# First input rows and first weights of the expert stage fetched ahead of the out projection's end

## The reference, cut to what matters

```python
    y = ys.transpose(1, 0, 2) + D_skip * xi
    y = y * jax.nn.silu(z)
    return y @ out_proj_w                      # the out projection
...
    h = residual + h
    residual = h
    h = rmsnorm(h, rms2_w)
    # moe_block: top 2 of 8 experts of each token
    for e in range(N_EXPERTS):
        w_e = jnp.where(sel == e, top_w, 0.0).sum(axis=-1)
        ye = jax.nn.silu(hs @ Wg[e]) * (hs @ Wu[e]) @ Wd[e]
        out = out + w_e[:, None] * ye
```

## Time and profile before

| | |
|---|---|
| median of 3 runs | 713.15 us (712.68 to 714.09) |
| the profiled execution, whole | 710.69 us |
| its span, first to last instruction | 708.9 us |
| busy: PE, DVE, ACT, POOL | 572.2, 483.9, 387.6, 324.7 us |
| mean granted clock of PE | 0.939 of 2.4 GHz |
| the chain that ended last | PE 40%, DVE 9%, issue 6%, ACT 4% of the span |

### The profile page before, as it was taken

How to read it: one execution, slowest core, us unless ns; L and a number is a source line. 1 busy time by engine, 2 the same in 40 slices (tenths; PEclk the granted TensorE clock), 3 DMA queues, 4 the chain that set the end, 5 groups by cost and what they waited for, 6 DMA issues and landing times.

```text
span 708.9 us, 11068 instructions
## 1 busy us (share of the span) xinstructions
PE 572.2 (81%) x3444; PEld 363.5 (51%) x3463; DVE 483.9 (68%) x1294; ACT 387.6 (55%) x618; POOL 324.7 (46%) x285
## 2 busy tenths in 40 slices
PE   3956889986795567788789999956789989988787
PEld 1412334442342222778789999933545545545466
DVE  4769999938999987444223655388687778887052
ACT  2675666666643553464356656523266566566741
POOL 5268989809895996225648332433012103112010
PEclk9979999997878988998899999976999999999999
DMA  5855556325774652300141201323103003000001
GB/s 146 292 168 158 156 167 190 113 63 177 235 224 148 177 164 67 87 19 32 46 117 34 82 21 32 108 82 81 35 2 106 10 3 106 3 3 1 3 15 46
DMA packets 50524, 65.92 MB, mean 93 GB/s; under 512 B 7730, under 2 KB 29250, under 8 KB 50210
## 3 DMA queue, kind: packets, MB, share of 16 engines
q1 hardware_dynamic: 45122, 59.27, 28.5%
q0 software_dynamic: 2496, 5.15, 2.0%
q10 hardware_dynamic: 2848, 0.78, 0.5%
HBM read 47.46 MB, written 9.52 MB: 80 GB/s over the span
## 4 chain that ended last, share of the span: by engine, by line
PE 40%; DVE 9%; issue 6%; ACT 4%; another core or an unknown queue 1%; ACTq 1%; POOL 0%; DMA 0%; POOLq 0%; DVEq 0%
PE ps L1643 37%; DVE arena L1563 3%; ACT arena L1163 2%; PE ps L1957 1%; DVE x L1498 1%; DVE nb L1262 1%; DVE stats L1249 1%; PE ps L1964 1%; PE ps L1847 1%; ACTq L1153 1%; ACT arena L1183 0%; ACT r L1163 0%; ACT arena L1171 0%; DVE mv L1252 0%
## 5 line engine op out<-in xcount | busy, mean ns | idle before, releaser
L1643 PE MATMUL ps<-arena 128*128 128x128 f32 (+12 forms) x2147 | 336.2, 333 | 53.5 <-DVE arena L1563 17.9
L1643 PEld LDWEIGHTS ps<-arena 128*128 128x128 f32 (+4 forms) x2166 | 214.6, 160 | 142.4 <-issue 65.1
L1643 PE MATMUL ps<-arena,ident 128*128 128x512 f32 x256 | 134.0, 664 | 46.4 <-DVE arena L1446 46.4
L1434 DVE TENSOR_TENSOR_SCAN arena<-ps,arena 128x512 f32<-128x512 f32 x128 | 149.4, 1211 | 13.3 <-ACT ps L1091 6.8
L859 POOL TENSOR_TENSOR arena<-arena 128x1024 f32<-128x1024 f32 x64 | 126.9, 1998 | 40.8 <-DVE arena L1421 38.4
L1091 ACT ACTIVATE ps<-arena 128x512 f32<-128x512 f32 x128 | 87.5, 690 | 79.3 <-DVE arena L1434 74.3
L1563 DVE CUSTOM_DVE_ANT_0 arena<-ps,cmask 128x128 f32<-128x128 f32 (+3 forms) x256 | 111.5, 488 | 26.5 <-PE ps L1643 25.4
L1643 PEld LDWEIGHTS ps<-arena,ident 128*128 128x128 f32 x256 | 51.5, 211 | 123.1 <-DVE arena L1446 68.3
L1617 DVE TENSOR_TENSOR arena<-arena,ps 128x512 f32<-128x512 f32 x46 | 31.7, 689 | 78.0 <-PE ps L1643 35.8
L846 POOL DMA_INDIRECT moe_out<-arena,xT x46 | 45.5, 988 | 82.7 <-DVE arena L1587 72.3
L1163 ACT ACTIVATE arena<-ps 128x1024 f32<-128x1024 f32 (+3 forms) x86 | 57.1, 709 | 36.0 <-PE ps L1643 35.6
(11 more groups left out here) (200 smaller groups left out, 609.9 us busy)
## 6 DMA issues: line engine op xcount, KB each, us to landing
arena<-bc_rows SPq DMA_DIRECT2D x128, 256.0 KB, 3.7
arena<-arena SPq DMA_DIRECT2D x64, 64.0 KB
arena<-arena SPq DMA_DIRECT2D x28, 128.0 KB, 2.4
moe_rows<-arena SPq DMA_DIRECT2D x2, 1495.0 KB, 11.9
arena<-moe_rows SPq DMA_DIRECT2D x8, 325.0 KB, 4.2
arena<-in_L_attn_a_Wg SPq DMA_DIRECT2D x8, 256.0 KB, 4.4
arena<-in_L_attn_a_Wu SPq DMA_DIRECT2D x8, 256.0 KB, 5.0
arena<-moe_out SPq DMA_DIRECT2D x4, 512.0 KB, 4.4
```

What stands on the lines that cost most here:

```text
L1434: V.tensor_tensor_scan(hst[:, g % STATES, e, :], bank(6 + e), dBx[:, g % RING, e, :], 0.0, ALU.mult, ALU.add).then_inc(s_scan, 1)
L1643: return T.matmul(o, l, rr, start=start, stop=stop)
```

## The change

Four things are done.

- `load_blocks(0)` no longer waits for `s_op` ahead of its first two transfers (blocks 0 to 7), but for `s_dx` at 4 and `s_ys` at 49, the last reads of `xc`, whose memory these blocks fill. From the third transfer on it waits for `s_op` as before. `load_blocks(1)` loses the wait for `s_op`, which stands ahead of it on the queue.
- ACT copies the first block's weights once all products with C are done (`s_hc`, `s_hp`), since these were the last reads of the scan states.
- `out_proj(1, block_turn)` turns block 0 between its two sequences and block 1 behind the second.
- The two turns behind the out projection are gone; the wait for the experts' weights stays and now stands ahead of PE's register load.

```diff
@@ -191,6 +191,7 @@
         CH = (0, 3, 8, 13, 18, NBLK)
+        EARLY = 2
@@ -268,6 +269,7 @@
         xg0 = carve([NBLK, NROW])
+        assert rows_at + CH[EARLY] * NROW <= moe_from + CT * HL
@@ -698,9 +700,13 @@
             def load_blocks(h):
-                sp.wait_ge(s_op, NB)
                 sp.wait_ge(s_sc[h], 16 * 2 * TH)
+                if h == 0:
+                    sp.wait_ge(s_dx, NB)
+                    sp.wait_ge(s_ys, NST - NS + 1)
                 for q in range(len(CH) - 1):
+                    if h == 0 and q == EARLY:
+                        sp.wait_ge(s_op, NB)
                     sp.dma_start(xg[h][:, CH[q]:CH[q + 1], :],
@@ -1202,7 +1208,8 @@
                 if i == 0:
-                    act.wait_ge(s_op, NB)
+                    act.wait_ge(s_hc, len(on_dve))
+                    act.wait_ge(s_hp, len(on_pool))
                     act.wait_ge(s_wg, 16 * (2 * NE + 1))
@@ -1698,7 +1705,7 @@
-            def out_proj(h):
+            def out_proj(h, behind=None):
                 pe.wait_ge(s_yg, 2 * h + 2)
@@ -1706,6 +1713,8 @@
                     last.then_inc(s_op, 1)
+                    if behind:
+                        behind(c)
@@ -1827,17 +1836,6 @@
-            out_proj(1)
...
+            out_proj(1, block_turn)
...
             pe.wait_ge(s_wg, 16 * (2 * NE + 1))
-            block_turn(0)
-            block_turn(1)
```

More of the change, by code:

```diff
@@ L1828, in _, with block_turn @@
                 sum_up(end - 1)
-            out_proj(1)
+            def block_turn(i):
+                h, k = divmod(i, NBLK)
+                for q in range(len(CH) - 1):
+                    if k == CH[q]:
+                        pe.wait_ge(s_xg[h][q], 16)
+                wait(pe, s_xh, i)
+                T.transpose(ps[:, 5, 0:P], xg[h][:, k, 0:D], ident[:]).then_inc(s_xt, 1)
+            out_proj(1, block_turn)
             def turn_last(c):
@@ L1839, in rank_last @@
                 rank(HB - 1)
[L1841 to L1847, removed]
             def gate_up(i):
```

## The result

The changed kernel takes 710.32 us (median of 20 runs, 707.29 to 712.15) where the kernel before takes 713.16 us (median of 20). The ratio is 0.9958, with a 95% interval of 0.9947 to 0.9969: 3.0 us faster, between 2.2 and 3.8. The forecast was 709.0 us, 4.2 us faster, in a range from 707.2 to 711.3. Two later measurements of the same kernel gave 0.9950 (0.9925 to 0.9974) and 0.9947 (0.9931 to 0.9964). The profiled execution took 707.9 us, with a span of 706.1; that before took 710.69 and 708.9. One execution of a later version (the split alone) took 948.22 us at a mean granted clock of 0.559 and isn't counted in its ratio.

What follows compares the result with a forecast made beforehand. TensorE was taken to wait for a load behind the out projection, then run slow-clocked. Of 5.4 to 6.0 us, h2's wait leaves 4.35, less 0.15: 713.15 - 4.2, about 709.0 us; range 707.2 to 711.3, own range 708.0 to 710.3.

Steps and rivals of the forecast that it cites:

- What bounds the kernel here: Behind the out projection, TensorE waits for a 2.57 us load asked for only then; 4.46 us hold 0.63 us of work.
- The early rows: Half 0's first loads: SP issues at 279.1, blocks land at 281.6, asked for at 285.7; margin 4.1 us.
- The early weights: ACT's 1.05 us copy of the first weights starts near 280.5, ends at 281.6; worth nothing by itself.
- The turn in the middle: Block 0's turn between the out projection's halves delays its end by 0.11 us, bounds 0.11 and 0.30.
- The register load: TensorE loading the expert's number before block 0's gate and up: an idle 0 to 0.64 us.
- The clock holds: TensorE's clock stays at 1.00 from 284 to 300 despite new idle times of about 0.5 and 1.0 us.
- the rival with 12%: Gaps at 292 and 293 drop the clock; one block's 16 records run at 1.2 GHz: 710.8 us, chance 12%.
- The price of a fall: Block 0's gate and up at the slow clock: 3.63 us against 1.79, so 1.84 us more.
- What is late next: Turn of h2 waits for POOL's power and `nb` rows until 294.1; 4.35 us kept, TensorE idle about 1.0.
- The saving is given back behind 327 us: POOL's scatters pace later blocks, so early blocks wait: saved 0 to 1.4 us, 711.8 to 713.2; chance 8%.
- The early turn stands and waits: Late rows stall the out projection's second half, each us late costing one us: 714.5 us, slower, chance 6%.
- the clock rival: TensorE's clock falls in the new gaps at 292 and 293, giving 1.84 us back: 710.8 us, chance 12%.

Runs made afterwards that it cites:

- the split alone: Changed kernel with the second half's residual, moments and power done one sequence after the other, POOL's memsets left in place: 0.9935 of the kernel before.
- the early rows alone: Kernel before with only the early loads of blocks 0 to 7; first weights' copy late, both turns behind the out projection: 0.9962 of the kernel before.
- the gap filled: Kernel before with 24 unread turns of the identity between out projection and first block's turn, all waits kept: 0.9987 of the kernel before.
- memsets moved: Changed kernel with POOL's two memsets held until VectorE has written the eight rows of `nb`: 0.9958 of the kernel before.
- Made real: Changed kernel with the first loads waiting until the first sequence's out projection is done (`s_op` at 3): 716.57 us, 1.0029 of the kernel before.
- the early rows with fillers: Kernel before with only early loads, weights late, both turns behind the out projection, 14 unread identity turns between them: 0.9955 of the kernel before.

## Why the prediction was right, and where its sizes were off

**What bounds the kernel here**: right. The load of the rows stood in the gap, and with it gone the gap closed.

**The early rows**: right. SP issued at 279.17 (forecast 279.1), the first turn found its rows, and the margin carried.

**The early weights**, "worth nothing by itself": the reason given doesn't carry. They were hidden behind the load, but the load was going. Left where they were, with both turns behind the out projection, they made the next gap and the clock fell, 1.47 us in the traces; what they would cost with the turn in the middle is open. I named the cover and didn't price its going. The sum wasn't hurt, since the weights are early in the change.

**The turn in the middle**: 0.11 us, right. The last step of the residual's moments starts 7.46 us from the out projection's start, and 7.36 before. The register load (0 to 0.64) cost nothing here; with both turns behind, an idle 0.75 us stands at its place again.

**The clock holds**: right, and the rival with 12% didn't come. The runs show how near it was. In the changed kernel idle times of 0.55 and 1.48 us with eight records between them left the clock at 1.00; in the version with the early rows alone 1.39 and 0.75 us with one turn between them didn't. The sentence that I took from the Trainium skill (TensorE: Matmul & The Clock Gate, "A second HAM failure mode: psum-queue depth-cycling") tells of a clock that swings to and fro under frequent short idle times. No trace of this passage shows that: the change's stays at 1.00, and the early rows alone show one fall behind two idle times. The price of a fall, 1.84 us, was too high. It set the 3.63 us of a row against the 1.79 of a step in the chain, and the two are measured differently; from start to start it is 3.47 against 1.86 with the gap filled, 1.61 us.

**What is late next**: right in kind, the chain of h2, and this is where the sum was 0.9 us too high for the passage. The terms, each from the start of the out projection:

| term | forecast | measured | off by |
|---|---|---|---|
| POOL's power done, VectorE starts `nb` | 9.40 us | 9.43 us | 0.03 |
| four rows and release, memsets aside | 0.92 us | 1.02 us (memsets moved) | 0.10 |
| the memsets' share in these rows | 0 | 11.80 - 11.24 = 0.56 us | 0.56 |
| turn of h2 to block 2's gate, above the stream's 0.44 | 0.15 us | 0.78 - 0.44 = 0.34 us | 0.19 |

The four sum to 0.88, and 4.2 - 0.88 = 3.32 us, where the passage's gain is 3.31. The step that failed is "VectorE then writes eight rows of `nb` in 1.66 us, the four of the first sequence in 0.83". The row was true for a VectorE that worked alone. I had moved it by 3 us without asking what stood on the other engines at the new time, and POOL's two memsets directly behind its power were in the trace of the kernel before (293.03 and 293.50, above). They wait for `s_op`, stand behind the power on POOL's list, and so run exactly when `nb` is written.

**The saving is given back behind 327 us**: no. The ranks and POOL's first scatter are earlier by all of 3.1 us, and the span by 2.8.

**The early turn stands and waits**: it didn't. Made real, it cost the delay, as said, and 1.68 us for the clock, which the price of one us for each us leaves out.

The median's 3.0 us (2.2 to 3.8) and the passage's 3.3 agree, and the forecast's 4.2 lies outside the interval. The measured 710.32 us is nearer to the clock rival's 710.8 than to 709.0; by the time alone the rival could not be told from a forecast that was too high, and it is the trace, with its clock of 1.00, that decides. It also lies just above the forecast's own range. That range doesn't follow from its terms: 0.19 us for the turn and 0.6 either way give 708.4 to 709.8, not 708.0 to 710.3.

## What to carry to other kernels

When a wait goes, find the chain that ends next to it and shorten that too: here the change gave 3.0 us, and taking the residual's chain apart by sequence (with the memsets moved) 2.29 us more in the traces and about 2 in the times, while by the traces the turn placed into the middle of the out projection was worth nothing until then. Reading a duration from the trace holds only beside the neighbours that it had; for a step that moves, look at what the other engines do at its new time. And an edit whose work is hidden can still be worth its clock: idle times of 1.39 and 0.75 us with one turn between them cost TensorE half its rate for the block behind, and idle times of 0.46 and 0.75 us didn't.

## What the runs showed that I had not expected

- VectorE's rows of `nb` (128x128, read from `r`, scaled by a column, written to `nb`) take 281 to 286 ns alone and up to 994 ns while POOL fills 512 elements of bf16 per partition. The memsets can be slow too: in the run with the split alone they took 0.61 and 0.67 us instead of 0.51. What the two engines contend for no run here shows.
- The passage of the changed kernel is 11.80, 11.81 and 11.81 us in three executions, while their whole times are 707.9, 709.94 and 710.55 us. The spread comes from elsewhere. Of the 2.7 us between the spans of the first and the third (706.1 and 708.8), 1.5 lie ahead of the out projection's start (283.93 and 285.42), 0.1 between it and the first scatter of half 1, and 1.1 behind that.
- The stage behind the ranks is another source. From block 2's gate to the first scatter of half 1 it took between 27.15 and 29.88 us in the 14 traces. The shortest, that of the early rows with fillers, is the only one whose clock stays at 1.00 there.
- A stall of 2.85 us in the middle of the out projection cost 4.7 us in the passage, because the clock fell behind it on work that others wait for.
